# Parts of three, three and two batches instead of two, three and three, in a one-core attention and expert layer

## The reference

```python
x = L0_attn_x                                   # (8, 512, 128) float32
x = x + attention(layernorm(x))                 # 16 heads, causal softmax, projection Wp
x = x + ffn(layernorm(x))

# ffn: a shared expert for every token, and 2 of 8 routed experts
shared = (silu(x @ shared_gate.T) * (x @ shared_up.T)) @ shared_down.T
probs = sigmoid(x @ router_w.T + routing_bias)
scores, indices = top_k(probs, 2);  scores = scores / sum(scores)
combined[t] = sum over its 2 experts e of score * ((silu(x @ gate_w[e]) * (x @ up_w[e])) @ down_w[e])
ffn = shared + combined
```

## Time and profile before

| | |
|---|---|
| time, median of 3 runs | 763.5 us (761.47 to 769.78) |
| the profiled execution's own time | 763.39 us |
| its span, first to last instruction | 761.6 us |
| granted TensorE clock, mean | 0.968 of full speed |
| busy: PE, DVE, ACT, POOL | 85%, 72%, 60%, 41% |
| attention ends (last masks on POOL) | 554 us |
| last matmul starts | 731 us |

### The profile page before, as it was taken

One profiled execution on the slowest core, in us unless ns is written; L12 is line 12 of the kernel. 1 busy time (PEld: TensorE's weight loads), 2 busy tenths in 40 slices (PEclk: granted clock), 3 DMA queues, 4 the chain that ended last, 5 costly groups with the idle time before them and its releaser, 6 DMA issues. The chain is left out here.

```text
span 761.6 us, 16417 instructions
## 1 busy us (share of the span) xinstructions
PE 646.7 (85%) x5426; PEld 393.1 (52%) x5426; DVE 551.7 (72%) x1932; ACT 453.7 (60%) x808; POOL 315.4 (41%) x515
## 2 busy tenths in 40 slices
PE   7466999999999988999999988899997788888920
PEld 6244455554554444455455445455476667577620
DVE  6688778688878788778868878867247755667862
ACT  3334676666767756677767665656785645555710
POOL 3492542123223226722322323666400066656573
PEclk9699999999999999999999999999999999999975
DMA  8200335523111201221111211132425653755332
GB/s 232 67 0 2 88 108 147 154 74 105 44 41 51 57 31 64 86 65 36 44 48 49 64 33 37 37 77 80 100 74 125 123 109 105 156 95 133 94 105 73
DMA packets 106881, 61.14 MB, mean 80 GB/s; under 512 B 47992, under 2 KB 98576, under 8 KB 106800
## 3 DMA queue, kind: packets, MB, share of 16 engines
q1 hardware_dynamic: 70368, 29.40, 16.1%
q10 hardware_dynamic: 32336, 22.29, 9.7%
q0 software_dynamic: 4096, 8.40, 4.1%
HBM read 19.95 MB, written 31.06 MB: 67 GB/s over the span
## 5 line engine op out<-in xcount | busy, mean ns | idle before, releaser
L1348 DVE CUSTOM_DVE_ANT_0 junk<-bank,causal 128x512 bf16<-128x512 f32 (+3 forms) x512 | 222.2, 483 | 54.7 <-PE bank L975 52.1
L1232 ACT ACTIVATE p_sb<-bank,inv_scale 128x512 f32<-128x512 f32 (+1 forms) x384 | 221.7, 614 | 40.4 <-PE bank L998 33.8
L885 POOL TENSOR_SCALAR_AFFINE_SELECT p_sb<-p_sb 128x384 f32<-128x384 f32 x128 | 67.0, 524 | 297.9 <-ACT p_sb L1232 297.6
L975 PE MATMUL bank<-ah,qh 128*128 128x512 f16 (+3 forms) x512 | 132.5, 303 | 41.3 <-DVE low L1348 37.1
L997 PE MATMUL bank<-ql,ah 128*128 128x512 f16 (+3 forms) x512 | 153.4, 300 | 0.0
L998 PE MATMUL bank<-qh,al 128*128 128x512 f16 (+3 forms) x512 | 152.9, 300 | 0.0
L996 PE MATMUL bank<-qh,ah 128*128 128x512 f16 (+3 forms) x512 | 147.1, 300 | 0.9 <-ACT p_sb L1232 0.9
L1201 ACT ACTIVATE qh<-bank 128x512 f16<-128x512 f32 x128 | 76.4, 597 | 87.2 <-PE bank L941 83.3
L1319 DVE TENSOR_TENSOR ql<-bank,qh 128x512 f16<-128x512 f32 x128 | 88.3, 690 | 43.6 <-ACT qh L1201 39.0
L975 PEld LDWEIGHTS bank<-ah,qh 128*128 128x128 f16 x512 | 50.1, 98 | 98.5 <-DVE low L1348 63.4
L1522 DVE SCALAR_TENSOR_TENSOR al<-bank,gu_scale,ah 128x512 f32<-128x512 f32 x69 | 51.6, 747 | 56.7 <-ACT ah L1264 36.4
(11 more groups left out here) (230 smaller groups left out, 1139.4 us busy)
## 6 DMA issues: line engine op xcount, KB each, us to landing
o_dram<-oT ACTq DMA_DIRECT2D x32, 256.0 KB
ys_dram<-ql ACTq DMA_DIRECT2D x25, 256.0 KB
xs_dram<-causal ACTq DMA_DIRECT2D x6, 832.0 KB, 4.6
wst<-in_Wkqv SPq DMA_DIRECT2D x8, 264.0 KB, 4.7
x_sb<-in_x SPq DMA_DIRECT2D x8, 256.0 KB, 5.9
o_all<-o_dram SPq DMA_DIRECT2D x8, 256.0 KB
r_all<-r_dram SPq DMA_DIRECT2D x8, 256.0 KB, 3.2
x_dram<-rows SPq DMA_DIRECT2D x8, 256.0 KB, 2.4
```

Source lines behind the costliest of these rows:

```text
L885: nc.gpsimd.affine_select(out=three, in_=three, compare_op=ALU.is_ge, fill=0.0, base=0, pattern=[[0, 3], [1, P]], channel_multiplier=-1).t ...
L975: last = nc.tensor.matmul(m.psum[M_BANK[n % 2]][:, at:at + w], qh[:, u % RING, i * P:(i + 1) * P], m.ah[:, seg(b, N, w)], start=True, stop ...
L1232: nc.scalar.activation(p_sb[v % P_RING][:, S_AT[k]:S_AT[k] + S_WIDTH[k]], m.psum[S_BANK[k]][:, 0:S_WIDTH[k]], ACT.Exp, scale=m.inv_scale[: ...
L1348: last = nc.vector.tensor_tensor_reduce(out=junk[:, (3 * u + k) % 2, at:at + w], in0=m.psum[M_BANK[(3 * u + k) % 2]][:, at:at + w], in1=m. ...
```

## The change

```diff
-SPLITS = ((0, 8), (8, 20), (20, 32))
+SPLITS = ((0, 12), (12, 24), (24, 32))
```

## The result

The changed kernel took 762.4 us (759.92 to 765.09, 20 runs) beside 764.14 us (760.81 to 769.78) for the kernel before: a ratio of 0.9965, 95% interval 0.995 to 0.9981. By the ratio that is 2.7 us less where 7.9 were forecast (by the interval, 1.5 to 3.8). The profiled execution took 761.1 us, its span is 759.4 us, the mean granted clock 0.968 as before.

The account below looks back on a forecast made before the run. PE's order of slots sets the pace until about 730 us, then POOL's fetches in the tail. 763.39 - 10.0 - 2.5 - 3.0 + 5.4 + 2.2 = 755.5 us profiled; forecast 755.6 us (763.5 - 7.9), range 749.5 to 762.

Parts of the forecast that it names:

- The tail (-10.0): Last part: 24 fetches become 16, so the last addition waits for an earlier landing, 10.0 us less.
- rival C: Tail held by another engine: PE's last shared result comes later, batch 7 starts 4.2 us later, 759.8 us; chance 0.15.
- POOL's queue in slots 129 to 135 (+5.4): End of attention: 12 sends, masks and `hn` fill POOL's queue, so the last mask ends later; 0 to +7.
- Rival A: End of attention: POOL keeps up, as ACT's and PE's waits are longer than seen; 750.2 us, chance 0.13.
- rival D: Slots 129 to 145: sends are dear where work is dense, 769.6 us, slower than before; chance 0.07.
- Routing beside attention (-3.0): Part 1's place group moves to where no head follows (-2.3), fewer sends beside heads (-0.7); between -3.5 and -2.
- The sends of slots 138 to 145 (+2.2): Behind attention: 12 sends slow 8 units by 0.28 us each; ends 0 and 4.2.
- rival B: Units behind attention: sends don't slow them; 753.4 us, chance 0.12.
- The start of part 2 (-2.5): Around units 38 to 44: part 2's late loads in a row go, as sends end 13 slots ahead; other end 0.
- the case worked out for its upper end: Whole kernel: rival C with the start of part 2 gaining nothing, 762.3 us.
- My theory of stops and falls: Behind attention, from the experiments: transfers stop PE, the clock falls to 1.2 GHz for 3.4 us; 1 to 2 us each.
- The rule of ports: Sends of slots 138 to 145: by separate memory ports their term would be 0 and the sum 2.2 lower.

Follow-up runs that it names:

- first pair: The first profiled runs of the kernel before and the changed kernel, unedited: 764.14 and 762.4 us, ratio 0.9965.
- second kind: Name for chips 5 and 2, where the kernel before takes 747 us; a lasting state instead of a chip property isn't excluded.
- first kind: Name for chips 8 and 4, where the kernel before takes 765 to 769 us; a lasting state instead of a chip property isn't excluded.
- before_third: The kernel before, nothing edited, run for its trace on chip 4 (first kind): span 766.4 us.
- after_third: The changed kernel, nothing edited, on chip 8 (first kind): ratio 0.994 to the kernel before.
- before_fourth: The kernel before, nothing edited, on chip 2 (second kind): 747.08 us, span 745.6 us.
- before: The kernel before, nothing edited, in the first pair: 764.14 us.
- before_again: The kernel before, nothing edited, on chip 8 (first kind): 765.77 us, span 766.6 us.
- three_fetches: The changed kernel with 3 of its 64 fetches, the first of each part, on chip 4 (first kind): ratio 0.9621 to the kernel before.
- up_in_halves: The changed kernel with every 256-column up matmul of the routed units made as two of 128, chip 8: ratio 1.0105 to the kernel before.
- no_sends_138_145_b: The changed kernel without the 12 sends of slots 138 to 145, on chip 4 (first kind): ratio 0.9915 to the kernel before.
- after: The changed kernel, nothing edited, in the first pair: 762.4 us, ratio 0.9965 to the kernel before.
- after_again: The changed kernel, nothing edited, on chip 5 (second kind): 736.8 us beside 747.18 for the kernel before, ratio 0.9852.
- after_fourth: The changed kernel, nothing edited, on chip 8 (first kind) in a later set: ratio 0.9977 to the kernel before.

## Why the prediction was wrong

**The tail (-10.0)** was right: 9.95 us in the first pair, 9.9 on the second kind (34.0 to 24.1), 8.7 as an edit of its own. On the first kind rival C's mechanism exists, the last shared result coming later than the last landing, but in both kernels. DVE's timeline of `before_third`:

```profile
755.00 0.75 DVE L1517 SCALAR_TENSOR_TENSOR x_sb<-bank,inv_down,x_sb 128x512 f32<-128x512 f32 x1 [18.71 <-remote]
```

On chips 8 and 4 the end is thus held by PE and not by POOL's row (the last fetch of `before_third` starts at 750.38 us), and the column of the tail shrinks by 13 us, from 42 to 29, not by 10. It doesn't eat the gain, but it is another path than the forecast's. PE's last products there come once POOL's row has ended (below), so a shorter row frees them too; that is my reading, no run tried it alone.

**POOL's queue in slots 129 to 135 (+5.4)** was right: +5.3 and +4.9 in the pairs, and without the sends 4.4 us in the trace and 5.8 in the medians. Rival A is excluded. (Its upper end was added up wrongly: with 1.40 us and the pause for each send, as rival D has it, it is +10.6 and not +7.) **Routing beside attention (-3.0)** fits the first pair (-2.8), but the start of head 127 scatters by over 2 us among traces of one kernel, so it is not confirmed beyond that.

**The sends of slots 138 to 145 (+2.2)** is the first step that failed. The sum took 8 units at 0.28 us, from unit 1 on. Four of the 12 sends stand ahead of unit 1, where it had no price at all. In the first pair they cost 2.1 us there; units 1 to 9 cost 2.0, as forecast; and units 9 to 14, which no send touches, cost 1.7 more, with a fall of the granted clock (see below). Together that is 5.7 us up to unit 14 (40.8 against 35.1). Up to unit 9 the five traces of the first kind with these 12 sends in place and matmuls unchanged took 3.8 to 5.8 us more than the kernel before (23.75 to 25.76 against 19.95), and the one without them 0.2 us less. On the second kind the sends cost nothing (36.4 against 36.5). I had taken the pace of 2.29 us for a property of the kernel. So rival B (sends don't slow the units) is what happens on the second kind, and on the first D's dear sends behind attention, at a third to a half of its 11.0 us. What PE looks like then, TensorE's timeline of `after_third` in the tail:

```profile
744.70 0.31 PE L1117 MATMUL bank<-wl,qh 128*128 128x128 f16 x1
745.95 0.27 PE L1115 MATMUL bank<-wh,qh 128*128 128x128 f16 x1 [0.94 <-issue]
747.34 0.26 PE L1116 MATMUL bank<-wh,qh 128*128 128x128 f16 x1 [1.12 <-issue]
748.03 0.27 PE L1117 MATMUL bank<-wl,qh 128*128 128x128 f16 x1 [0.43 <-issue]
748.76 0.27 PE L1115 MATMUL bank<-wh,qh 128*128 128x128 f16 x1 [0.46 <-issue]
749.48 0.28 PE L1116 MATMUL bank<-wh,qh 128*128 128x128 f16 x1 [0.45 <-issue]
750.17 0.26 PE L1117 MATMUL bank<-wl,qh 128*128 128x128 f16 x1 [0.41 <-issue]
751.58 0.28 PE L1115 MATMUL bank<-wh,qh 128*128 128x128 f16 x1 [1.15 <-issue]
752.27 0.28 PE L1116 MATMUL bank<-wh,qh 128*128 128x128 f16 x1 [0.42 <-issue]
752.35 0.31 PE L1117 MATMUL bank<-wl,qh 128*128 128x128 f16 x1
752.46 0.31 PE L1115 MATMUL bank<-wh,qh 128*128 128x128 f16 x1
```

and POOL's timeline beside it, the last fetch:

```profile
748.94 0.95 POOL L919 DMA_INDIRECT p_sb<-ys_dram,place  x1 [0.30 <-issue]
```

No wait stands behind these gaps ("issue"), PE's matmuls come 0.7 or 1.4 us apart instead of 0.1, and some 2.4 us after POOL's last transfer has been issued they run on at 0.08 to 0.11. The weight loads between them come late as well, and take no longer for it (0.10 us), so a slow load isn't what the matmuls wait for:

```profile
746.64 0.10 PEld L1116 LDWEIGHTS bank<-wh,qh 128*128 128x128 f16 x1 [1.29 <-issue]
747.34 0.10 PEld L1117 LDWEIGHTS bank<-wl,qh 128*128 128x128 f16 x1 [0.60 <-issue]
748.74 0.10 PEld L1115 LDWEIGHTS bank<-wh,qh 128*128 128x128 f16 x1 [1.29 <-issue]
```

In the waits of PE between 612 and 705 us the kernel before has such gaps on chip 4 and none on chip 2. From `before_third`:

```profile
PE bank L1079 <- issue: 5.3, 9, 1.9
PE bank L1080 <- issue: 3.2, 8, 0.9
PE bank L1117 <- issue: 2.0, 3, 1.0
PE bank L1116 <- issue: 1.4, 3, 0.5
PE bank L1081 <- issue: 1.2, 4, 0.4
PE bank L1115 <- issue: 0.4, 1, 0.4
```

The same view of `before_fourth` has no line with "issue". The matmuls themselves are no slower: those of L1079 over 256 columns took 276 ns in the mean in `before_third` and 280 in `before_fourth`, between the same two times.

**The start of part 2 (-2.5)** is the second. The forecast gave the late loads a price without looking for the wait. On the first kind PE doesn't wait for them: the view above of `before_third`, and the same view of `before` and of `before_again`, has no line in which PE waits for a transfer, where that of `before_fourth` has 5.6 us. In `before_fourth` POOL issues the 24 sends nearly in a row (from 612.88 to 643.49 us), SP can start loading at 646.52, and unit 39's silu stands at 644.95 us, so PE waits. In `before` POOL itself waits for PE between sends (from 612.59 to 648.69), the load starts at 651.50 us, and unit 38 only comes at 653.53. So the order was worth 7.7 us on the second kind, and on the first nothing to speak of: from unit 24 to 44 it is 48.3 to 49.0 us before and 48.4 to 51.3 after.

What kept units 24 to 44 slow on the first kind is POOL's transfers, of which 30 stand beside them before and 30 now. The forecast had them cost the same before and after. The change moves them: 20 stood beside units 24 to 38 and 10 beside 38 to 44, now it is 22 and 8, 12 of the 22 being fetches (2 before). Units 24 to 38 took 31.6 to 32.0 us before and 34.7 to 36.5 now, and 30.3 in `three_fetches`: without 11 of those 12 fetches 4 to 6 us less. Why 22 transfers cost so much more there than 20 did isn't shown; in the changed kernel these are routed units nearly throughout (24 to 37), where the kernel before has shared ones from 34 on, with half as many up matmuls, and `up_in_halves` shows that more instructions cost more. That part is argued.

**A step that was missing:** reading part 1's words moved with the part's begin, from a slot in which PE waits for DVE to one in which it doesn't. Unit 16's slot grew from 1.99 to 3.80 us in the first pair, and on the second kind from 1.98 to 3.92, where units 14 to 24 took 29.5 us instead of 26.2 (the other 1.4 us lie in units 20 and 21 and were not followed up). With the words put back (and parts of four, two and two) it took 27.1: about 2.4 us there, and 1.6 or more on chip 4.

**The sums.** From left to right in the table, the first pair gives -3.8 (routing) +5.3 (queue) +5.7 (sends) +0.7 (units 14 to 24) -0.7 (part 2) +0.5 -10.0 (tail) = -2.3, beside -2.2 by the spans. Of the 5.6 us between that and the forecast's -7.9, 3.5 are the sends, 1.8 part 2, 0.7 units 14 to 24 and 0.5 units 44 to 66, less 0.8 at head 127 (where the two traces already differed by 1.0 at head 0) and 0.1 in the queue. With the means of three traces of each kernel on the first kind it is -4.2 +5.4 +6.2 +0.9 +1.3 -0.1 -12.1 = -2.6, as the spans say, beside -1.8 to -4.6 by the ratios (times 765). The second kind's traces give -0.6 +4.9 -0.1 +3.3 -7.6 +0.0 -9.9 = -10.0, as the spans say (745.6 and 735.6). That this lies near the forecast is luck: part 2 gave 5 us more than forecast, units 14 to 24 took 3.3 that it had at nothing, the sends cost 2.3 less than forecast, and head 127 gained 2.4 less. The two large terms, tail and queue, had the right mechanism and size in the first pair and on the second kind. The two mid-sized ones were priced from stretches that are slow beside transfers on the first kind alone.

The range went up to 762, though the case worked out for its upper end was 762.3. The 762.4 measured lies above both.

**The clock.** My theory of stops and falls was half right. Falls of the granted clock to 1.2 GHz come in all traces, and units 9 to 14 show their price: 15.1 us where none falls there (`before`, `before_third`, `no_sends_138_145_b`), 16.4 to 16.8 in most where one does. That is about 1.5 us each, and they stand in traces of both kinds, of the kernel before too (16.6 in `before_again` and `before_fourth`). From the windows of `after` and of `after_again`:

```profile
565.00:575.00 10.00, 7.65 (x71) 6.19 (x69) 6.84 (x11) 7.28 (x12) 4.78 (x5) 0.83 0.49 125
```

```profile
565.00:575.00 10.00, 8.88 (x103) 7.70 (x101) 7.63 (x13) 8.56 (x15) 4.98 (x6) 1.00 0.49 136
```

The clock is the third column from the right: 0.83 means that it stood at half for a third of the 10 us. This one fall (units 3 to 5) explains at most 1.7 of the 5.7 us, half of its 3.4. But units 1 to 5, which took 9.5 us with it and 7.4 in the kernel before, took 9.2 in `three_fetches` and 9.8 in `after_fourth` with the clock at full speed, so it explains next to nothing there. A second fall, in units 12 and 13 of `after`, goes with the 1.7 us that units 9 to 14 took more.

**The rule of ports.** The Trainium skill (SBUF — State Buffer, "SBUF: two separate sides") says that engines and transfers have ports of their own and can't slow each other. The second kind agrees: a unit takes 1.98 us beside transfers (27.7 us for 14), and the same without them in `three_fetches`. On the first kind units are slowed beside transfers, so of the time measured there "can't slow each other" does not hold. What the traces show is instructions that come late and not slower matmuls (276 ns and 280 ns, above), so nothing here speaks against what it says of ports.

## What stays open

Why two kinds of chip differ in this; what PE's instructions wait for there; why attention, with the same transfers beside matmuls of 512 columns, shows so little (1.0 us for 24 sends by the forecast's rows; its longer matmuls need fewer instructions, but no run tried others there); and on the first kind the split of what is left of the loss between units 24 and 44, and the price of the sends beside units 14 to 24, which no run left out. Whether the falls of the clock follow the stops was not tried apart from them.

## What to carry to other kernels

A stretch that is slow beside transfers is no property of the kernel until a second chip has shown it: here 18 us of 765 were the chip's, and a term read from such a stretch came out at -0.1 or at +4 to +6. When a term is priced per unit, look also at the transfers that stand ahead of the first unit counted: four of 12 sends did, for 2 to 3 us. Before a late load is given a price, look for the wait that it causes: on the first kind there was none. Where part of the work moves, list the small reads that are tied to its begin; they sat in the shadow of a wait and came out of it for 2 us. And a gain behind a queue (POOL's 24 sends) must be worked out against the pace of the engine that will wait, since a slower engine hides it.

## What the hardware showed unexpectedly

- On the first kind, beside transfers that GpSimd issues in a row, TensorE's instructions come at times 0.7 us apart (0.06 to 0.11 otherwise), worth 6 to 8 us in 14 units (33.9 to 35.6 instead of 27.7). DVE waited up to 18.7 us for the last shared result. Twice the instructions for the same columns: 5.0 us more in 14 units. On the second kind the units kept 27.7 us beside the same transfers, and no such gap stands there.
- An indirect send costs GpSimd 0.96 us and a pause of 0.30 on both kinds.
- A fall of the granted clock to half, 3.4 us long, cost about 1.5 us in units 9 to 14 on the first kind (15.1 us without, 16.4 to 16.8 with). On the second kind every trace has one there, at 16.5 to 16.8 us.
